# A quarter of the pair products laid with the batch on the partitions and summed by ScalarE and GpSimd

## The chip, the cores and the metric

The kernel runs on one core of a Trainium2 chip. The time is the device time of one execution in microseconds (us). The kernel before was timed at a median of 256.03 us over three runs (255.77 to 256.83). The profile is one more execution on the chip, with the instructions, DMA packets and semaphore events of that core.

## What is computed

It is a recommendation tower. For each of 512 samples, 32 table rows of 64 numbers are looked up. Each of the 496 pairs of fields has its own 64x64 matrix, and the pair gives one number per sample. These 496 numbers go through a linear layer, and then through a small network.

```python
e = jnp.stack([tbl_0[ids[:, 0]], ..., tbl_31[ids[:, 31]]], axis=1)      # 512 x 32 x 64
p = e[:, rows, :]; q = e[:, cols, :]                                    # rows, cols = triu_indices(32, k=1)
pij = jnp.einsum('bpe,dpe,bpd->bp', p, kernel, q)                       # kernel: 64 x 496 x 64, pij: 512 x 496
z = pij @ W.T + b                                                       # 256 wide
h = jnp.concatenate([z, dense_ctx], axis=1)                             # 272 wide
h = jnp.maximum(h @ W_top1 + b_top1, 0.0)                               # 512 wide
h = jnp.maximum(h @ W_top2 + b_top2, 0.0)                               # 256 wide
y = h @ W_top3
```

## The kernel before

**Layout.** The 32 fields are taken two at a time as 16 chunks. In `x_sb` a chunk is 128 partitions (two fields of 64 features) by 512 samples. Fields of chunks 0 to 3 come from small tables and are picked by one-hot matmuls (line 322), whose one-hots VectorE and ScalarE build (lines 543, 460, 463). The rows of chunks 4 to 15 are gathered by GpSimd with indirect DMAs into `gathered`, with 128 samples on the partitions: eight gathers for a chunk, 96 in all (line 280). After each of them GpSimd runs a memset of `rest_sb` (line 287), and it waits until the gather before the last has landed. TensorE then turns a chunk with four transposes (line 334, `turn`), and ScalarE copies it to `x_sb` and `own_sb` (lines 482, 486).

**The product groups.** The pairs are cut into tiles of two pairs and into 124 groups of two tiles. A group takes two matmuls (lines 351, 352), one on the upper and one on the lower half of the array rows, with the pair matrices in `k_sb` as the weights and 512 samples of `x_sb` as the moving operand. They fill one of three double banks of `t_ps`. VectorE multiplies the bank by `x_sb` of the other field into `prod` (line 556), a ring of six. Each such product still has to be summed over 64 features, which lie on the partitions. So after every four groups (`RUN`) TensorE runs two `reduce` calls of four matmuls (line 372) with a 0/1 selector; they accumulate in `sum_ps`. Every 16 such calls make a window, which ScalarE keeps in `pair_sums` (line 468). Four groups, those of fields inside a set of four chunks, have four smaller matmuls instead (lines 355 to 360).

**The order.** `plan()` writes out one order of steps, "fill c" (bring in chunk c) and "group g", and each engine walks it. TensorE works strictly in that order: a `turn` whose rows have not landed holds every group behind it, also those of earlier chunks. Chunk c is turned up to `LEAD` = 3 groups before its first group. The chunks' first groups are 7, 11, 16, 22, 30, 38, 47, 57, 69, 81, 94 and 108 for chunks 4 to 15. After the last group come the linear layer (line 379), the last two reduce calls, and the network (lines 405 to 431).

A product may start when VectorE has finished with the bank three products back (`prod_ready`), and the pieces of `k_sb` are loaded by SyncE, paced by the gathers.

Of the kernel before, what the change touches and what calls it, by code (L numbers as in the profile page):

```python
# [10 lines left out]
ALU = mybir.AluOpType  # L11
ACT = mybir.ActivationFunctionType

P = 128
# [31 lines left out]
GROUP = []  # L46
for c in range(CHUNKS):
    across = [(c, False, [[(i, 2 * c), (i, 2 * c + 1)] for i in (2 * a, 2 * a + 1)]) for a in range(c)]
    within = [(c, True, [[(2 * a + 1, 2 * a), (2 * a + 2, 2 * a + 3)] for a in (c - 3, c - 1)])] if c % SET == SET - 1 else []
    at = (1 - len(GROUP)) % RUN  # L50
    GROUP += across[:at] + within + across[at:]
GROUPS = len(GROUP)
NT = 2 * GROUPS
WITHIN = [g for g in range(GROUPS) if GROUP[g][1]]
FIRST_GROUP = [min(g for g in range(GROUPS) if GROUP[g][0] == c) if c else 0 for c in range(CHUNKS)]

BLOCK, BLOCK_OF = [], []
for g, (_, within, tiles) in enumerate(GROUP):  # L60
# [15 lines left out]
REDUCES = NT // COLS  # L76
# [4 lines left out]
G_RING = 8  # L81
LEAD = 3
# [19 lines left out]
def plan():  # L102

    steps, chunks = [], 0
    for g in range(GROUPS):
        while chunks < CHUNKS and (chunks < max(2, ONE_HOTS) or g >= FIRST_GROUP[chunks] - min(LEAD, (chunks - 1) // 2)):
            steps.append(("fill", chunks))
            chunks += 1
        steps.append(("group", g))
    return steps  # L110


def build(nc, ids, ids_t, iota, pick, tables, kern, w_pairs, b_int, ctx_rows, w_ctx_rows, w1, b1, w2, b2, w3, ident, selector, out):
    steps = plan()
    with ExitStack() as ctx:
# [18 lines left out]
        pair_sums = sb("pair_sums", [P, WINS, BATCH])  # L134

# [69 lines left out]
        window_kept = sem("window_kept")  # L205
        z_done = sem("z_done")
# [60 lines left out]
        def _(pool):  # L267
            pool.memset(w3_wide[:], 0.0).then_inc(w3_cleared, 1)
            pool.wait_ge(ids_in, 16)
            for n in range(CHUNKS - ONE_HOTS):  # L270
                if n >= G_RING:
                    pool.wait_ge(filled, n - G_RING + ONE_HOTS + 1)
                for f in range(2):
                    field = FIELD[2 * (n + ONE_HOTS) + f]
                    for t in range(BT):
                        k = (2 * n + f) * BT + t
                        landed = k - FLIGHT
                        if landed >= 0:
# [8 lines left out]
                        pool.memset(rest_sb[:], 0.0).then_inc(rested, 1)  # L287

        @block.tensor
        def _(pe):  # L290
# [35 lines left out]
            def turn(c):  # L326
# [6 lines left out]
                for t in range(BT):  # L333
                    mm = pe.transpose(tp_ps[:, t * P:(t + 1) * P], gathered[:, n % G_RING, t], ident_sb[:])  # L334
# [295 lines left out]
```

## Time and profile before

| | |
|---|---|
| Median of three runs | 256.03 us (255.77 to 256.83) |
| Profiled execution | 255.97 us |
| Its span, first to last instruction | 254.2 us |
| TensorE busy | 243.8 us, 96% |
| VectorE busy | 183.6 us, 72% |
| ScalarE busy | 50.5 us, 20% |
| GpSimd busy | 136.9 us, 54% |

The 1.77 us between the execution and its span lie around the first and the last instruction. The span has three parts: the picks with one-hots up to about 44 us, the product groups from there to 226.3 us, and the layers to the end. PE is TensorE, PEld its weight loads, DVE VectorE, ACT ScalarE and POOL GpSimd. The idle time of an engine counts only if another one, or the end, waits for it.

### The profile page before, as it was taken

To read this page: it belongs to the slowest core of one execution; us is meant where nothing else is said; L and a number is where in the kernel's file an instruction comes from. 1 tells how busy PE (TensorE), PEld (TensorE's weight loads), DVE (VectorE), ACT (ScalarE), POOL (GpSimd) and SP (SyncE) were. 2 spreads that over 40 slices of the span, in tenths; PEclk is the share of its full clock that TensorE was granted. 3 is DMA by queue.
4 is the path that set the end of the run, shared out by engine and by line. 5 is a ranking of instruction groups with operands and counts; after the bars stand their busy time and mean duration, and the time that the engine had idled before them with its cause. 6 is when DMAs were issued, how large, how long until landed. Compare 5 with 4: busy or idle time off the path is not lost.

```text
span 254.2 us, 3686 instructions
## 1 busy us (share of the span) xinstructions
PE 243.8 (96%) x1378; PEld 93.8 (37%) x1378; DVE 183.6 (72%) x205; ACT 50.5 (20%) x86; POOL 136.9 (54%) x197
## 2 busy tenths in 40 slices
PE   7778799999999999999999999999999999999996
PEld 3443454333332333333323333333333323333474
DVE  1999996867778687887768788788778768870130
ACT  3768677111110102010100200100100100001121
POOL 5766988888888888878888878700000000000000
PEclk9799999999999999999999999999999999999999
DMA  6294322333323333333333331182000000000000
GB/s 168 57 279 114 83 60 73 82 85 81 76 77 78 86 84 75 77 77 83 83 75 83 72 84 34 21 274 49 0 1 3 0 0 3 0 0 0 0 3 0
DMA packets 11028, 16.38 MB, mean 64 GB/s; under 512 B 5166, under 2 KB 5810, under 8 KB 11010
## 3 DMA queue, kind: packets, MB, share of 16 engines
q1 hardware_dynamic: 7768, 12.97, 18.0%
q0 software_dynamic: 3072, 3.15, 6.8%
q8 instruction: 11, 0.18, 0.3%
q10 hardware_dynamic: 170, 0.03, 0.1%
q14 instruction: 7, 0.06, 0.1%
HBM read 16.13 MB, written 0.00 MB: 63 GB/s over the span
## 4 chain that ended last, share of the span: by engine, by line
PE 91%; ACT 3%; issue 3%; DVE 2%; DVEq 0%
PE t_ps L351 43%; PE sum_ps L372 23%; PE sum_ps L322 5%; PE tp_ps L322 3%; PE t_ps L412 3%; PE tp_ps L334 3%; ACT distance L460 2%; PE t_ps L355 2%; PE t_ps L359 2%; PE tp_ps L379 2%; PE sum_ps L295 1%; PE t_ps L421 1%; PE t_ps L379 1%; PE t_ps L352 1%; ACT own_sb L486 1%
## 5 line engine op out<-in xcount | busy, mean ns | idle before, releaser
L556 DVE TENSOR_TENSOR prod<-t_ps,x_sb 128x1024 f32<-128x1024 f32 x120 | 139.3, 1218 | 33.4 <-PE t_ps L352 32.8
L351 PE MATMUL t_ps<-x_sb,k_sb 64*128 64x512 f32 x240 | 113.4, 606 | 0.4 <-ACT own_sb L486 0.4
L352 PE MATMUL t_ps<-x_sb,k_sb 64*128 64x512 f32 x240 | 113.5, 607 | 0.0
L280 POOL DMA_INDIRECT gathered<-in_tbl,ids_sb x96 | 94.7, 987 | 26.8 <-issue 13.0
L351 PEld LDWEIGHTS t_ps<-x_sb,k_sb 64*128 64x128 f32 x240 | 41.4, 186 | 63.1 <-issue 37.6
L372 PE MATMUL sum_ps<-prod,sel_sb 128*32 128x512 f32 x496 | 59.6, 598 | 0.0
L287 POOL MEMSET rest_sb<- 128x380 f32 x96 | 42.0, 438 | 0.1
L352 PEld LDWEIGHTS t_ps<-x_sb,k_sb 64*128 64x128 f32 x240 | 41.4, 186 | 0.0
L482 ACT COPY x_sb<-tp_ps 128x512 f32<-128x512 f32 x14 | 8.2, 586 | 107.1 <-PE tp_ps L334 104.2
L372 PEld LDWEIGHTS sum_ps<-prod,sel_sb 128*32 128x32 f32 x496 | 12.9, 109 | 42.3 <-issue 21.3
L543 DVE TENSOR_SCALAR pair_sums<-ids_bc,iota_sb 125x512 bf16<-125x512 f16 x57 | 24.3, 488 | 2.5 <-ACT ids_bc L444 2.1
L322 PE MATMUL tp_ps<-pair_sums,k_sb 125*64 125x512 bf16 x72 | 16.1, 411 | 4.3 <-DVE pair_sums L543 1.5
L322 PE MATMUL sum_ps<-pair_sums,k_sb 125*64 125x512 bf16 x76 | 14.6, 382 | 1.7 <-DVE pair_sums L543 1.0
L468 ACT COPY pair_sums<-sum_ps 128x512 f32<-128x512 f32 x4 | 2.3, 585 | 68.7 <-PE sum_ps L372 68.7
L460 ACT ACTIVATE distance<-ids_bc,iota_sb 125x512 f16<-125x512 f16 x17 | 12.1, 713 | 1.8 <-PE tp_ps L322 1.7
L463 ACT ACTIVATE pair_sums<-distance 125x512 bf16<-125x512 f16 x17 | 10.7, 630 | 0.5
L556 DVE TENSOR_TENSOR prod<-t_ps,own_sb 128x1024 f32<-128x1024 f32 x4 | 4.9, 1224 | 8.1 <-PE t_ps L360 8.1
L322 PEld LDWEIGHTS tp_ps<-pair_sums,k_sb 125*64 125x64 bf16 x72 | 6.7, 116 | 10.8 <-DVE pair_sums L543 3.4
L322 PE MATMUL tp_ps<-pair_sums,prod 125*64 125x512 bf16 x36 | 10.2, 411 | 0.0
L322 PE MATMUL sum_ps<-pair_sums,prod 125*64 125x512 bf16 x38 | 9.2, 379 | 0.0
L322 PEld LDWEIGHTS sum_ps<-pair_sums,k_sb 125*64 125x64 bf16 x76 | 5.8, 109 | 7.7 <-ACT pair_sums L463 2.2
L334 PEld LDWEIGHTS tp_ps<-ident_sb,gathered 128*128 128x128 f32 x48 | 5.0, 140 | 9.5 <-issue 9.5
(56 smaller groups left out, 117.5 us busy)
## 6 DMA issues: line engine op xcount, KB each, us to landing
k_sb<-in_kern SPq DMA_DIRECT2D x112, 64.0 KB, 2.1
gathered<-in_tbl,ids_sb POOLq DMA_INDIRECT x96, 2.6
k_sb<-in_tbl SPq DMA_DIRECT2D x5, 280.0 KB
k_sb<-in_kern SPq DMA_DIRECT2D x4, 256.0 KB, 4.0
w_sb<-in_w SPq DMA_DIRECT2D x2, 512.0 KB, 5.0
k_sb<-in_tbl SPq DMA_DIRECT2D x3, 224.0 KB
w_pairs_sb<-in_w_pairs SPq DMA_DIRECT2D x1, 512.0 KB, 3.4
ctx_sb<-in_ctx_rows SPq DMA_DIRECT2D x1, 192.0 KB, 5.5
```

The source lines that it names most:

```text
L280: pool.indirect_dma_start(gathered[:, n % G_RING, t, f * EMB:(f + 1) * EMB], None, tables[field], bass.IndirectOffsetOnAxis(ap=ids_sb[:, t ...
L287: pool.memset(rest_sb[:], 0.0).then_inc(rested, 1)
L322: mm = pe.matmul(bank[half:half + EMB, :], part[:, f, r, :], one_hot[:, n % OH_RING, :], start=(r == 0 and part is high_sb), stop=(r == PI ...
L334: mm = pe.transpose(tp_ps[:, t * P:(t + 1) * P], gathered[:, n % G_RING, t], ident_sb[:])
L351: pe.matmul(t[:, 0, :], k_sb[low, k, :], x_sb[low, a, :], start=True, stop=True)
L352: pe.matmul(t[:, 1, :], k_sb[high, k, :], x_sb[high, a, :], start=True, stop=True).then_inc(t_ready, 1)
L372: mm = pe.matmul(sum_ps[32 * j:32 * j + 32, :], sel_sb[:, 30 - 2 * k:62 - 2 * k], prod[:, (t // 2) % PROD_RING, t % 2, :], start=(k == 0), ...
L460: act.activation(distance[:, k % 2, :], ids_bc[:, f, :], ACT.Abs, scale=-1.0, bias=iota_sb[:, PICK[f][1] + r:PICK[f][1] + r + 1]).then_inc ...
L463: act.activation(one_hot[:, n % OH_RING, :], distance[:, k % 2, :], ACT.Relu, scale=-1.0, bias=1.0).then_inc(one_hot_ready_a, 1)
L482: act.copy(x_sb[:, n, :], from_ps[:]).then_inc(x_ready, 1)
L543: dve.tensor_scalar(one_hot[:, n % OH_RING, :], ids_bc[:, f, :], iota_sb[:, PICK[f][1] + r:PICK[f][1] + r + 1], None, ALU.is_equal).then_i ...
L556: dve.tensor_tensor(prod[:, g % PROD_RING], t_ps[:, g % T_RING], q, ALU.mult).then_inc(prod_ready, 1)
```

## The change

Chunks 4 to 7 are called near, chunks 0, 1 and 8 to 13 far. The pairs of a near with a far chunk, 32 of the 120 chunk pairs, leave the groups and become 32 side units: one for each far chunk and each quarter of the batch. In a side unit the operands of the matmuls change places. The weights are 128 samples of `x_sb`, and the moving operand is four blocks of `k_sb`, 512 columns. The result has the batch on the partitions. VectorE multiplies it by the near chunks' rows as gathered, which for that reason stay in four slots of `gathered` for good; the later chunks share the other four (`gathered_slot`), so a gather now waits for the turn of four chunks back. The features then lie along the free dimension, so no reduce matmul is needed. They are summed in `side_prod`, a ring of three: for 18 units by ScalarE with 16 ACTIVATEs that have an accumulator output (`sum_side`), for 14 of the last 20 by GpSimd with six halving additions, behind all its gathers. The sums of all units, 128 columns for each quarter, are turned once (`turn_side_sums`), just ahead of the last group, and kept in `pair_sums`.

So there are 92 groups and 32 side units, and 46 reduce calls where there were 62. The side units stand one behind every fourth group from group 15 on, and from group 62 on four among five groups. The first groups of chunks 4 to 15 are now 7, 9, 12, 16, 22, 26, 31, 37, 45, 53, 62 and 76, and `LEAD` is 5.

```diff
+NEAR = [4, 5, 6, 7]
+FAR = [0, 1, 8, 9, 10, 11, 12, 13]
...
+LEAD = 5
+SIDE_AT = [g for g in range(15, 63, RUN)] + [62 + 5 * k // 4 for k in range(SIDE_UNITS - 12)]
+SIDE = [(c, t) for c in FAR for t in range(BT)]
+BY_POOL = [m for m in range(12, SIDE_UNITS) if m % 3 != 2]
+BY_ACT_SUM = [m for m in range(SIDE_UNITS) if m not in BY_POOL]
+def plan():
+    steps, chunks, side = [], 0, 0
+    for g in range(GROUPS):
+        while chunks < CHUNKS and (chunks < max(2, ONE_HOTS) or g >= FIRST_GROUP[chunks] - min(LEAD, (chunks - 1) // 2)):
+            steps.append(("fill", chunks))
+            chunks += 1
+        steps.append(("group", g))
+        while side < SIDE_UNITS and SIDE_AT[side] <= g:
+            steps.append(("side", side))
+            side += 1
+        if g == GROUPS - 2:
+            steps.append(("side sums", 0))
+    return steps
...
-REDUCES = NT // COLS
+REDUCES = 2 * GROUPS // COLS
-G_RING = 8
-LEAD = 3
+G_RING = len(NEAR) + 4
+SIDE_RING = 3
+def gathered_slot(n):
+    return n if n < len(NEAR) else len(NEAR) + (n - len(NEAR)) % (G_RING - len(NEAR))
@@ gpsimd
-                    pool.wait_ge(filled, n - G_RING + ONE_HOTS + 1)
+                    pool.wait_ge(filled, n - (G_RING - len(NEAR)) + ONE_HOTS + 1)
+            halvings = 0
+            for m in BY_POOL:
+                c, t = SIDE[m]
+                k = FAR.index(c)
+                pool.wait_ge(prod_ready, UNITS.index(("side", m)) + 1)
+                part = side_prod[:, m % SIDE_RING].rearrange("p s (n e) -> p (s n) e", e=EMB)
+                for width in (32, 16, 8, 4, 2):
+                    if halvings:
+                        pool.wait_ge(halved, halvings)
+                    pool.tensor_tensor(part[:, :, 0:width], part[:, :, 0:width], part[:, :, width:2 * width],
+                                       ALU.add).then_inc(halved, 1)
+                    halvings += 1
+                pool.wait_ge(halved, halvings)
+                pool.tensor_tensor(side_sums[:, t, 16 * k:16 * k + 16], part[:, :, 0], part[:, :, 1],
+                                   ALU.add).then_inc(side_summed_p, 1)
@@ tensor
+            def side_products(m):
+                c, quarter = SIDE[m]
+                u = UNITS.index(("side", m))
+                k = SIDE_BLOCK_OF[c]
+                if quarter == 0:
+                    weights_in(k, len(NEAR))
+                    pe.wait_ge(x_ready, 2 * (c + 1))
+                pe.wait_ge(prod_ready, u - T_RING + 1)
+                t = t_ps[:, u % T_RING]
+                cols = slice(quarter * P, (quarter + 1) * P)
+                low, high = slice(0, EMB), slice(EMB, P)
+                pe.matmul(t[:, 0, :], x_sb[low, c, cols], k_sb[low, k:k + len(NEAR), :].rearrange("p g m -> p (g m)"),
+                          start=True, stop=True)
+                pe.matmul(t[:, 1, :], x_sb[high, c, cols], k_sb[high, k:k + len(NEAR), :].rearrange("p g m -> p (g m)"),
+                          start=True, stop=True).then_inc(t_ready, 1)
+            def turn_side_sums():
+                pe.wait_ge(side_summed_a, len(BY_ACT_SUM))
+                pe.wait_ge(side_summed_p, len(BY_POOL))
+                pe.wait_ge(x_ready, 2 * CHUNKS)
+                for t in range(BT):
+                    mm = pe.transpose(tp_ps[:, t * P:(t + 1) * P], side_sums[:, t, :], ident_sb[:])
+                mm.then_inc(side_turned, 1)
@@ scalar
+            def sum_side(m):
+                c, t = SIDE[m]
+                k = FAR.index(c)
+                act.wait_ge(prod_ready, UNITS.index(("side", m)) + 1)
+                for n in range(16):
+                    part = side_prod[:, m % SIDE_RING, n // 8, n % 8 * EMB:(n % 8 + 1) * EMB]
+                    one = act.activation(part, part, ACT.Copy, accum_out=side_sums[:, t, 16 * k + n:16 * k + n + 1])
+                one.then_inc(side_summed_a, 1)
@@ vector
+                if kind == "side":
+                    t = SIDE[g][1]
+                    if g >= SIDE_RING:
+                        user = g - SIDE_RING
+                        if user in BY_POOL:
+                            dve.wait_ge(side_summed_p, BY_POOL.index(user) + 1)
+                        else:
+                            dve.wait_ge(side_summed_a, BY_ACT_SUM.index(user) + 1)
+                    q = gathered[:, 0:len(NEAR), t, :].rearrange("p (o c) n -> p o c n", o=1)
+                    dve.tensor_tensor(side_prod[:, g % SIDE_RING].rearrange("p s (c n) -> p s c n", c=len(NEAR)),
+                                      t_ps[:, u % T_RING].rearrange("p s (c n) -> p s c n", c=len(NEAR)),
+                                      q.broadcast_to([P, 2, len(NEAR), P]), ALU.mult).then_inc(prod_ready, 1)
+                    continue
```

TensorE in the kernel before, the last stretch ahead of the turn of chunk 9 (the L334 row); L351 with L352 is one group, L372 x8 are two reduce calls:

```order
231 L351 MATMUL t_ps<-x_sb,k_sb 128x512
232 L352 MATMUL t_ps<-x_sb,k_sb 128x512
233 L351 MATMUL t_ps<-x_sb,k_sb 128x512
234 L352 MATMUL t_ps<-x_sb,k_sb 128x512
235 L351 MATMUL t_ps<-x_sb,k_sb 128x512
236 L352 MATMUL t_ps<-x_sb,k_sb 128x512
237 L351 MATMUL t_ps<-x_sb,k_sb 128x512
238 L352 MATMUL t_ps<-x_sb,k_sb 128x512
239 L372 MATMUL sum_ps<-prod,sel_sb 32x512 x8
240 L351 MATMUL t_ps<-x_sb,k_sb 128x512
241 L352 MATMUL t_ps<-x_sb,k_sb 128x512
242 L334 MATMUL tp_ps<-ident_sb,gathered 128x128 x4
```

There, 35 products stood ahead of this turn. TensorE in the changed kernel, from the turn of chunk 8 to that of chunk 9 (L413 is the turn, L460 and L461 a group, L434 and L436 a side unit, L481 the reduce calls):

```order
207 L413 MATMUL tp_ps<-ident_sb,gathered 128x128 x4
208 L460 MATMUL t_ps<-x_sb,k_sb 128x512
209 L461 MATMUL t_ps<-x_sb,k_sb 128x512
210 L434 MATMUL t_ps<-k_sb,x_sb 128x512
211 L436 MATMUL t_ps<-k_sb,x_sb 128x512
212 L460 MATMUL t_ps<-x_sb,k_sb 128x512
213 L461 MATMUL t_ps<-x_sb,k_sb 128x512
214 L460 MATMUL t_ps<-x_sb,k_sb 128x512
215 L461 MATMUL t_ps<-x_sb,k_sb 128x512
216 L481 MATMUL sum_ps<-prod,sel_sb 32x512 x8
217 L413 MATMUL tp_ps<-ident_sb,gathered 128x128 x4
```

Now four products, and no longer eight, lie between these two turns, and 24 stand ahead of the second. The turns of chunks 7, 8, 10, 11, 12, 13, 14 and 15 have 13, 20, 30, 37, 47, 57, 68 and 91 products ahead of them, where they had 19, 27, 44, 54, 66, 78, 91 and 105.

GpSimd's queue ended with a gather and a memset. In the changed kernel the halvings stand behind these; the first of them:

```order
197 L343 DMA gathered<-in_tbl,ids_sb 128x64
198 L350 MEMSET rest_sb 128x380
199 L361 ISA
200 L361 TENSOR_TENSOR side_prod<-side_prod 128x16x32
201 L361 TENSOR_TENSOR side_prod<-side_prod 128x16x16
202 L361 TENSOR_TENSOR side_prod<-side_prod 128x16x8
203 L361 TENSOR_TENSOR side_prod<-side_prod 128x16x4
204 L361 TENSOR_TENSOR side_prod<-side_prod 128x16x2
205 L365 TENSOR_TENSOR side_sums<-side_prod 128x16
```

Six additions are one side unit's sums, and 14 such sets stand there.

## Rows read from the trace of the kernel before

**Rows 1.** The page's first two parts: busy time, and 40 slices of the span.
```profile
PE 243.8 (96%) x1378; PEld 93.8 (37%) x1378; DVE 183.6 (72%) x205; ACT 50.5 (20%) x86; POOL 136.9 (54%) x197
...
PE   7778799999999999999999999999999999999996
...
PEclk9799999999999999999999999999999999999999
```

**Rows 2.** The chain that ended last, in order of time: start us, us, what.
```profile
106.30 1.85 PE sum_ps L372 x16
108.15 0.62 PE t_ps L351
108.78 0.42 PE t_ps L351
...
110.07 0.59 PE tp_ps L334 x4
...
112.57 1.85 PE sum_ps L372 x16
114.43 0.62 PE t_ps L351
...
118.06 1.85 PE sum_ps L372 x16
```

**Rows 3.** The same chain, turns of chunks 8, 9 and 11, a within group, and the last step.
```profile
80.76 0.57 PE t_ps L355
...
85.68 0.59 PE tp_ps L334 x4
...
97.45 0.59 PE tp_ps L334 x4
...
125.40 0.59 PE tp_ps L334 x4
...
226.31 2.77 PE tp_ps L379 x6
```

**Rows 4.** GpSimd's gathers (L280) alone, by stretches: us, POOL busy (gathers issued), PEclk, DMA.
```profile
0.00:61.50 61.50, 33.73 (x32) 0.97 0.42 109
0.00:86.90 86.90, 49.06 (x48) 0.98 0.39 100
0.00:99.30 99.30, 56.71 (x56) 0.98 0.39 98
0.00:112.90 112.90, 64.32 (x64) 0.98 0.38 96
0.00:125.40 125.40, 71.93 (x72) 0.99 0.37 94
```

**Rows 5.** GpSimd in order of time, and gathers from issue to landing (min, median, max).
```profile
84.26 0.95 POOL L280 DMA_INDIRECT gathered<-in_tbl,ids_sb  x1 [0.17 <-issue]
85.21 0.43 POOL L287 MEMSET rest_sb<- 128x380 f32 x1
86.01 0.95 POOL L280 DMA_INDIRECT gathered<-in_tbl,ids_sb  x1 [0.37 <-DMA gathered<-in_tbl,ids_sb]
...
111.90 0.95 POOL L280 DMA_INDIRECT gathered<-in_tbl,ids_sb  x1 [0.27 <-DMA gathered<-in_tbl,ids_sb]
...
DMA to landing us min/median/max: 2.4/2.6/6.1
```

**Rows 6.** VectorE in order of time: start us, us, what.
```profile
121.02 4.62 DVE L556 TENSOR_TENSOR prod<-t_ps,x_sb 128x1024 f32<-128x1024 f32 x4 [0.87 <-PE t_ps L352]
127.10 1.22 DVE L556 TENSOR_TENSOR prod<-t_ps,x_sb 128x1024 f32<-128x1024 f32 x1 [1.46 <-PE t_ps L352]
```

**Rows 7.** All engines by stretches: us, PE, PEld, DVE, ACT, POOL busy (instructions), PEclk.
```profile
8.00:9.00 1.00, 0.49 (x2) 0.32 (x3) 1.00 (x2) 1.00 (x4) 1.00 (x2) 0.83 0.00 0
9.00:12.00 3.00, 3.00 (x14) 1.62 (x13) 2.96 (x8) 2.02 (x4) 2.67 (x4) 0.50 0.14 22
12.00:15.00 3.00, 2.79 (x24) 1.77 (x21) 2.97 (x7) 2.49 (x4) 2.69 (x4) 0.99 0.83 246
251.00:254.20 3.20, 0.65 (x10) 0.39 (x8) 0.00 (x0) 0.27 (x1) 0.00 (x0) 1.00 0.00 1
```

**Rows 8.** Instructions by line and shape: count, busy us, mean ns of one, idle before.
```profile
L287 POOL MEMSET rest_sb<- 128x380 f32 x96 | 42.0, 438 | 0.1
L268 POOL MEMSET w_wide<- 128x64 f32 x1 | 0.2, 151 | 0.3 <-POOLq L622 0.3
L505 ACT COPY y_sb<-t_ps 128x128 f32<-128x128 f32 x1 | 0.3, 265 | 1.3 <-PE t_ps L431 1.3
L494 ACT COPY w_wide<-w_sb 128x2 f32<-128x2 f32 x1 | 0.2, 198 | 0.0
```

More of the change, by code:

```diff
@@ L41, with is_side, side_tile @@
 OH_RING = 8
-GROUP = []
+NEAR = [4, 5, 6, 7]
+FAR = [0, 1, 8, 9, 10, 11, 12, 13]
+SIDE_TILES = 8 * len(FAR)
+SIDE_GROUPS = SIDE_TILES // 2
+SIDE_UNITS = BT * len(FAR)
+def is_side(c, a):
+    return c in FAR and a in NEAR or c in NEAR and a in FAR
+def side_tile(k, s, n):
+    return 4 * (8 * (k % 2) + 4 * s + n) + k // 2
+side_tiles = {side_tile(k, s, n): [(2 * c + s, 2 * near), (2 * c + s, 2 * near + 1)]
+              for k, c in enumerate(FAR) for s in range(2) for n, near in enumerate(NEAR)}
@@ L51 @@
[L51 to L60, printed above, removed]
+    at = (1 - len(MAIN)) % RUN
+    MAIN += across[:at] + within + across[at:]
+GROUPS = len(MAIN)
+GROUP += MAIN
+NT = 2 * len(GROUP)
+WITHIN = [g for g in range(GROUPS) if MAIN[g][1]]
@@ new lines @@
+FIRST_GROUP = [min(g for g in range(GROUPS) if MAIN[g][0] == c) if c else 0 for c in range(CHUNKS)]
+LEAD = 5
[16 more added lines that the diff above has]
+    return steps
@@ new lines @@
+STEPS = plan()
+UNITS = [step for step in STEPS if step[0] in ("group", "side")]
+UNIT_OF_GROUP = [UNITS.index(("group", g)) for g in range(GROUPS)]
+BLOCK, BLOCK_OF, SIDE_BLOCK_OF = [], [], {}
+for kind, n in UNITS:
+    if kind == "side":
+        c, t = SIDE[n]
+        if t == 0:
+            SIDE_BLOCK_OF[c] = len(BLOCK)
+            BLOCK += [tuple((side_tile(FAR.index(c), s, k), (0, 1), 2 * c + s) for s in range(2)) for k in range(len(NEAR))]
+        continue
+    _, within, tiles = MAIN[n]
+    g = SIDE_GROUPS + n
@@ L99, in reduced_after @@
     return range(max(0, (g - RUN - 1) // 2), (g - 1) // 2) if g % RUN == 1 else range(0)
[L102 to L110, printed above, removed]
+def gathered_slot(n):
+    return n if n < len(NEAR) else len(NEAR) + (n - len(NEAR)) % (G_RING - len(NEAR))
 def build(nc, ids, ids_t, iota, pick, tables, kern, w_pairs, b_int, ctx_rows, w_ctx_rows, w1, b1, w2, b2, w3, ident, selector, out):
-    steps = plan()
+    steps = STEPS
     with ExitStack() as ctx:
@@ L333, in turn, with weights_in @@
                 for t in range(BT):
-                    mm = pe.transpose(tp_ps[:, t * P:(t + 1) * P], gathered[:, n % G_RING, t], ident_sb[:])
+                    mm = pe.transpose(tp_ps[:, t * P:(t + 1) * P], gathered[:, gathered_slot(n), t], ident_sb[:])
                 mm.then_inc(filled, 1)
+            def weights_in(k, blocks):
+                for s in range(SLICES):
+                    if k <= s * KS < k + blocks:
+                        pe.wait_ge(k_in[s], 16 * (2 if s < PIECES_FROM else PIECES))
@@ L339, in products @@
                 k = BLOCK_OF[g]
[L340 to L344 removed]
+                u = UNIT_OF_GROUP[g]
+                weights_in(k, 1 + within)
+                if u >= T_RING:
+                    pe.wait_ge(prod_ready, u - T_RING + 1)
                 if g == FIRST_GROUP[c]:
@@ L390, in _ @@
                         turn(n)
+                elif kind == "side":
+                    side_products(n)
+                elif kind == "side sums":
+                    turn_side_sums()
                 else:
```

61 lines of the change are left out of this document (37 added, 24 removed).

## The prediction

> **What bounds the kernel now.** I read the busy shares and slices first [rows 1]: TensorE is busy in every slice from the seventh to the last but one, at the full clock, so time is won only where TensorE loses work, and lost wherever it waits. Then the chain that ended last [rows 2]: TensorE alone, in a pattern. From one pair of reduce calls to the next without a turn it is 118.06 - 112.57 = 5.49 us, for four products. Inside, records follow at 0.43 us, two to a product, so a **product** is 0.857 us and four are 3.43. The **pair of reduce calls** is the rest, 2.06 us (1.85 of matmuls, and 0.20 by which the first record behind it, 0.62, is longer than the others' 0.42). With a turn the cycle is 112.57 - 106.30 = 6.27 us, so a **turn** is 0.78 us. VectorE needs 4.62 us for four multiplications in a row and 1.22 for one [rows 6], so they follow at 1.13 us. It fits four into 5.49 us and is not the bound. Last I read what feeds the turns, GpSimd's gathers [rows 4, 5]: they run from the start at a pace of their own, 0.95 us + 0.43 of memset + 0.17 and now and then a wait for a landing, some 13 us for a chunk's eight. At 86.9 us 48 are issued, which is chunks 4 to 9; the last of them went out at 86.01 and lands 2.6 us later, at about 88.7. TensorE turns chunk 9 at 97.45 [rows 3], 8.8 us later. So today the gathers are early, and that margin is not large.
>
> **What is saved.** Products: 32 groups go, 32 side units come, each again with two matmuls of 512 columns on half the rows, and I price one like a group, 0.857 us. Reduce calls: 62 become 46, eight pairs, 8 x 2.06 = 16.5 us off TensorE. The turn of the side sums adds 0.78. Taken alone, the span would be 254.2 - 16.5 + 0.8 = 238.5 us.
>
> **Where it goes: the turns come before their rows.** The order gives the products ahead of each turn. Chunk 9 has 24 ahead of it, where it had 35. In the kernel before, TensorE stood at product 24 shortly ahead of the within group at 80.8 us [rows 3]; now it has one turn more behind it at that point and short waits for the rows of chunks 7 and 8, so it arrives at about 82. The rows land at 88.7. Nothing in the change touches the pace of the gathers: the same 96, the same memsets, and the new wait for the turn of four chunks back is first met by chunk 12, for the turn of chunk 8, long past by then. **Chunk 9** holds TensorE 6.6 us, whatever happened before. From its turn (0.78, to 89.5) six products and one pair of reduce calls are 5.14 + 2.06, so TensorE stands at chunk 10 at 96.7; that chunk's last gather, the 56th, is issued by 99.3 [rows 4], about 98.5, and lands at 101.1: **4.4 us** of wait. To chunk 11 seven products and one pair, 0.78 + 6.00 + 2.06, so 109.9; its last gather went out at 111.90 and lands at 114.5: **4.6 us**. Chunk 12 comes ten products and two pairs later, a within group among them, at about 129.6, and its 72 gathers are all issued by 125.4 and landed by about 127; from there the rows are in time.
> So the turn of chunk 11 stands at 114.6 us. Before it was at 125.40, and 226.31 - 125.40 = 100.9 us later the groups were done [rows 3]; in these were 70 products, 17 pairs of reduce calls, five turns and two within groups. Now 87 products, 15 pairs, the same turns and within groups, and the turn of the side sums are left: 100.9 + 17 x 0.857 - 2 x 2.06 + 0.78 = 112.2 us. The groups end at 226.8 us: **0.5 us later than before**. The whole 16.5 us are spent in waits for rows.
>
> **The dense stretch.** From group 62 on, four side units stand among five groups, so seven products (once eight) lie between reduce pairs where there were four. TensorE makes one in 0.857, VectorE takes one in 1.13, and there are three banks. A pair of reduce calls lets VectorE catch up. Counted from its end, VectorE is done with the first product at 1.06 (0.857 and the longer start) + 0.1 + 1.22 = 2.4 us, and then every 1.13. TensorE needs a bank for its sixth product at 4.49 and gets it at 4.66, a wait of 0.17; the seventh and the eighth wait 0.27 each. Five stretches of 0.44 and one of 0.71 make 2.9 us, less where a turn lies between: **2.7 us**. Bounds: 0, if the three banks smooth it, and 5, if a multiplication by `gathered` with its broadcast takes 0.1 us more, which no row shows.
>
> **The clock.** The granted clock fell to its lower level (1.2 of 2.4 GHz) once in the kernel before, from about 8.7 to 12.1 us, behind a pause of 1.3 us and light work, and 9 to 12 us reads 0.50 [rows 7]. After the last matmul it stays at 1.00 to the end of the span. Pauses of 6.6, 4.4 and 4.6 us are none that a row shows, and I expect it to fall in the first and in the third. What is lost behind the first is taken back from the wait at chunk 10, but behind chunk 11 nothing absorbs it: 3.4 us at half rate cost **1.7 us**. Bounds 0 and 3.4 (twice the stretch). The Trainium skill, TensorE: Matmul & The Clock Gate, Part 1, says that the throttled state is the default and activity releases it; by this the fall is certain in the long pause, and the sum would stay as it is.
>
> **The sums.** No row shows an addition of GpSimd or an accumulating ACTIVATE. *GpSimd*: memsets of 380 and 64 elements take 438 and 151 ns [rows 8], so 0.91 ns an element and 93 ns fixed. Six additions write 512 + 256 + 128 + 64 + 32 + 16 = 1008 elements: 0.9 us, and six times 93 ns and a 0.17 us gap [rows 5], 1.6 us, make 2.5 us as the low end; with two reads and a write in turn, three times the element time, 4.3. I take 3.9, nearer the end that moves two operands. Three side units come with 6.75 products and 0.94 pairs of reduce calls, 8.0 us with small waits, and GpSimd has two of the three, so it keeps up to **4.0 us** a unit, and 3.9 is just covered by the products. The last two side units both belong to it; six products' time behind them is not quite enough for both: **0.6 us** at the turn of the side sums. Of GpSimd, the Trainium skill, GPSIMD Engine Reference, 3.1 and 4.1, says that a two-input elementwise operation is about twice as slow as on VectorE, and that one belongs there: 4.5 us for 2048 elements. By that figure a unit would be an estimated 3.8 us, the sum would be about the same, and the margin to 4.0 is that thin.
> *ScalarE*: copies of 128 and 2 columns take 265 and 198 ns [rows 8], so 64 columns about 232 ns. Sixteen are 3.7 us, and with a second instruction of 198 ns to bring out each accumulator 6.9. It gets one side unit in 6.35 us up to group 59, beside two copies of some 1.2 us for each chunk, so up to about 5.8 it costs nothing. I take 4.5, and nothing. At 6.9 it would cost 4 us.
>
> **The sum.** 254.2 + 0.5 + 2.7 + 1.7 + 0.6 = 259.7 us of span, and with the 1.77 around it **261.5 us**. The profiled execution (255.97) is as good as the median (256.03), so it stands as it is: +2.1%.
>
> **The rivals.**
> *The sums bind.* If a GpSimd unit takes 5 us, 14 of them are 70 us. The first starts when side unit 12 is multiplied, at about 169 us, so the last is done at 239; with the turn of the side sums and the last group the groups end at 241, where the forecast has 231.8: 9 us more, 271 us. It decides from 4.0 us a unit up; my price lies at 3.9, and the ring of three hands the delay to VectorE and then to TensorE. ScalarE at 7 us is the smaller form, 265. For it speaks how narrow both margins are, against it that the low ends lie well under them. Chance 0.22.
> *The waits for rows and little else.* VectorE's and the clock's terms vanish: 254.2 + 0.5, with 1.77 around it 256.5 us, no change that a measurement of this kernel can tell (about 0.5%). Chance 0.15.
> *The rows are in time*, and it is faster: the eight pairs are saved, the dense stretch costs its 2.7, so 238.5 + 2.7 + 1.8 = 243.0 us. The place is the turns of chunks 9 to 11, and it decides where GpSimd issues a chunk's gathers in under 8.5 us and not in 13. The pace of 1.55 us a gather does not depend on TensorE, so a gain of this size is hardly to be had; a pace a little quicker, less disturbed by landings (0.37 where a row shows it), would give 2 or 3 us. Chance 0.07 for all that ends under 254.7.
> The forecast, from 257.3 to 266, has the rest, 0.56.
>
> **How the numbers follow.** Likeliest is 261.5 us. The low end of the range, 256.0, takes in the case with the waits alone; the high end, 272, the known bounds together (5 for VectorE, 3.4 for the clock, 4 for ScalarE, some 3 for GpSimd at 4.3: 254.2 + 0.5 + 15.4 + 1.8 = 271.9) and part of the case in which the sums bind. Faster by over 0.5%: 0.07; within 0.5%: 0.14; slower: 0.79.
>
> **What the profile after would show.** Right: TensorE idle ahead of the turns of chunks 9, 10 and 11 by about 6.6, 4.4 and 4.6 us, released by gathers; the turn of chunk 11 at 114.6; an unchanged pace of gathers; 46 reduce calls; short waits for VectorE behind 165 us, and VectorE near 98% there; a lower clock around 89 or 115 us; the layers starting near 232. Wrong: turns of chunks 9 to 11 without idle time; a TensorE wait of many us at the side sums, or VectorE waiting for GpSimd, would mean that the sums bind; side units longer than 0.857 us would be a cost that I have put at nothing.

## The result, and the profile after

The changed kernel takes 263.2 us (median of four runs, 261.15 to 263.57) against 255.9 us (255.14 to 256.83): a ratio of 1.028, with a 95% interval of 1.024 to 1.032. It is slower. The profiled execution has a span of 261.4 us, 7.2 more than before.

The page's first two parts, as in [rows 1]:

```profile
PE 236.9 (91%) x1254; PEld 92.1 (35%) x1254; DVE 182.7 (70%) x205; ACT 120.8 (46%) x662; POOL 182.5 (70%) x281
...
PE   7788799998986395949999999999999999999996
...
PEclk9799999999999779979999999999999999999999
```

TensorE has 124 matmul records fewer and is busy 6.9 us less, but three notches stand in its row, between the 13th and the 18th slice (78 to 118 us), where the kernel before had none. The clock's row has notches behind the first and the last. TensorE in order of time around the turn of chunk 9 (start us, us, what, and in brackets the idle time and who ended it), and the part of all idle time ahead of the turns between 81 and 116 us:

```profile
81.02 1.92 PE L481 MATMUL sum_ps<-prod,sel_sb 128*32 128x512 f32 x16
89.00 1.08 PE L413 MATMUL tp_ps<-ident_sb,gathered 128*128 128x128 f32 x4 [6.05 <-DMA gathered<-in_tbl,ids_sb]
...
  DMA gathered<-in_tbl,ids_sb: 12.5, 3
```

These are the three waits at the turns of chunks 9 to 11, and they end with a gather's landing. Two short ones, of 1.0 and 0.7 us, stand at chunks 7 and 8. Answering to [rows 4], the gathers alone by stretches:

```profile
0.00:61.50 61.50, 33.15 (x31) 0.97 0.41 108
0.00:86.90 86.90, 48.83 (x48) 0.98 0.39 100
0.00:112.90 112.90, 64.14 (x64) 0.95 0.37 95
0.00:125.40 125.40, 71.31 (x72) 0.95 0.36 93
```

They are where they were, to one gather, so the rows arrive when they did before, and TensorE comes for them earlier. The chain that ended last says the same. Before, it was 91% TensorE; now it is this:

```profile
PE 55%; DMA 21%; POOL 19%; issue 4%; ACT 0%
PE t_ps L460 21%; DMA gathered<-in_tbl,ids_sb 20%; POOL gathered L343 13%; PE sum_ps L481 11%; PE t_ps L434 10%; POOL rest_sb L350 6%; PE t_ps L526 3%; PE tp_ps L488 1%; PE t_ps L535 1%; PE tp_ps L413 1%; PE t_ps L488 1%; PE t_ps L464 1%; PE t_ps L468 1%; DMA ids_sb<-in_ids 1%; PE tp_ps L535 1%
```

Up to the turn of chunk 11 the chain runs through GpSimd and its gathers, behind it through TensorE alone. It passes that turn at 114.99 us, and the layers start at 233.56 (226.31 before):

```profile
114.99 1.09 PE tp_ps L413 x4
...
161.09 1.85 PE sum_ps L481 x16
167.59 1.85 PE sum_ps L481 x16
176.35 1.85 PE sum_ps L481 x16
185.12 1.85 PE sum_ps L481 x16
...
229.00 1.85 PE sum_ps L481 x16
231.91 0.59 PE tp_ps L444 x4
233.56 2.77 PE tp_ps L488 x6
```

The clock, answering to [rows 7], by stretches (us, then PE, PEld, DVE, ACT, POOL busy, and PEclk):

```profile
84.00:88.00 4.00, 0.00 (x0) 0.00 (x0) 0.00 (x0) 0.88 (x8) 3.51 (x6) 0.96 0.35 88
88.00:94.00 6.00, 5.00 (x14) 2.58 (x16) 1.38 (x2) 1.17 (x2) 5.49 (x8) 0.50 0.32 77
...
115.00:118.00 3.00, 3.00 (x10) 1.64 (x12) 0.00 (x0) 2.98 (x21) 2.67 (x5) 0.50 0.28 68
118.00:120.00 2.00, 2.00 (x18) 0.54 (x18) 1.87 (x2) 0.24 (x1) 1.83 (x3) 0.91 0.42 105
```

And the new operations, by line and shape (mean ns of one behind the busy us):

```profile
L591 ACT ACTIVATE side_prod<-side_prod 128x64 f32<-128x64 f32 x288 | 69.1, 241 | 66.4 <-DVE side_prod L686 58.5
L591 ACT ACTIVATION_READ_ACCUMULATOR side_prod<-side_prod 128x1 f32 x288 | 53.9, 187 | 0.0
L686 DVE TENSOR_TENSOR side_prod<-t_ps,gathered 128x1024 f32<-128x1024 f32 x32 | 38.9, 1216 | 3.1 <-PE t_ps L436 3.1
L361 POOL TENSOR_TENSOR side_prod<-side_prod 128x512 f32<-128x512 f32 x14 | 17.8, 1272 | 15.0 <-DVE side_prod L686 15.0
L361 POOL TENSOR_TENSOR side_prod<-side_prod 128x256 f32<-128x256 f32 x14 | 10.3, 735 | 1.1
L365 POOL TENSOR_TENSOR side_sums<-side_prod 128x16 f32<-128x16 f32 x14 | 3.0, 217 | 1.1
```

The multiplication by `gathered` takes 1216 ns, as that by `x_sb` does. ScalarE and GpSimd sat waiting for VectorE for 58.5 and 15.0 us, and nobody is shown waiting for them.

### The profile page after: what moved, and what is told of

The parts are those of the page before. It is cut to its first block, busy times and chain, and to the rows that moved or that the text cites. A ratio compares the mean times of both kernels' runs of the same rounds, so it can differ in the third digit from the quotient of the medians.

```text
span 261.4 us, 4114 instructions
## 1 busy us (share of the span) xinstructions
PE 236.9 (91%) x1254; PEld 92.1 (35%) x1254; DVE 182.7 (70%) x205; ACT 120.8 (46%) x662; POOL 182.5 (70%) x281
## 4 chain that ended last, share of the span: by engine, by line
PE 55%; DMA 21%; POOL 19%; issue 4%; ACT 0%
PE t_ps L460 21%; DMA gathered<-in_tbl,ids_sb 20%; POOL gathered L343 13%; PE sum_ps L481 11%; PE t_ps L434 10%; POOL rest_sb L350 6%; PE t_ps L526 3%; PE tp_ps L488 1%; PE t_ps L535 1%; PE tp_ps L413 1%; PE t_ps L488 1%; PE t_ps L464 1%; PE t_ps L468 1%; DMA ids_sb<-in_ids 1%; PE tp_ps L535 1%
## 5 line engine op out<-in xcount | busy, mean ns | idle before, releaser
L699 DVE TENSOR_TENSOR prod<-t_ps,x_sb 128x1024 f32<-128x1024 f32 x88 | 104.4, 1217 | 39.0 <-PE t_ps L461 31.3
L591 ACT ACTIVATE side_prod<-side_prod 128x64 f32<-128x64 f32 x288 | 69.1, 241 | 66.4 <-DVE side_prod L686 58.5
L460 PE MATMUL t_ps<-x_sb,k_sb 64*128 64x512 f32 x176 | 92.0, 631 | 0.1
L461 PE MATMUL t_ps<-x_sb,k_sb 64*128 64x512 f32 x176 | 92.1, 632 | 0.0
L361 POOL TENSOR_TENSOR side_prod<-side_prod 128x512 f32<-128x512 f32 (+4 forms) x70 | 42.5, 607 | 19.4 <-DVE side_prod L686 15.0
L591 ACT ACTIVATION_READ_ACCUMULATOR side_prod<-side_prod 128x1 f32 x288 | 53.9, 187 | 0.0
L460 PEld LDWEIGHTS t_ps<-x_sb,k_sb 64*128 64x128 f32 x176 | 30.5, 192 | 48.5 <-issue 26.1
L481 PE MATMUL sum_ps<-prod,sel_sb 128*32 128x512 f32 x368 | 44.3, 598 | 0.0
L686 DVE TENSOR_TENSOR side_prod<-t_ps,gathered 128x1024 f32<-128x1024 f32 x32 | 38.9, 1216 | 3.1 <-PE t_ps L436 3.1
L434 PE MATMUL t_ps<-k_sb,x_sb 64*128 64x512 f32 x64 | 34.2, 614 | 0.0
L436 PE MATMUL t_ps<-k_sb,x_sb 64*128 64x512 f32 x64 | 34.2, 614 | 0.0
L461 PEld LDWEIGHTS t_ps<-x_sb,k_sb 64*128 64x128 f32 x176 | 30.5, 192 | 0.0
L413 PE MATMUL tp_ps<-ident_sb,gathered 128*128 128x128 f32 x48 | 8.7, 308 | 14.5 <-DMA gathered<-in_tbl,ids_sb 14.2
L481 PEld LDWEIGHTS sum_ps<-prod,sel_sb 128*32 128x32 f32 x368 | 9.6, 109 | 31.5 <-issue 24.3
L401 PE MATMUL tp_ps<-pair_sums,k_sb 125*64 125x512 bf16 x72 | 15.6, 410 | 3.9 <-DVE k_sb L652 1.5
L434 PEld LDWEIGHTS t_ps<-k_sb,x_sb 64*128 64x128 f32 x64 | 11.3, 190 | 19.3 <-issue 10.1
L413 PEld LDWEIGHTS tp_ps<-ident_sb,gathered 128*128 128x128 f32 x48 | 5.6, 153 | 24.1 <-issue 22.9
```

Source lines behind the costliest of these rows:

```text
L361: pool.tensor_tensor(part[:, :, 0:width], part[:, :, 0:width], part[:, :, width:2 * width], ALU.add).then_inc(halved, 1)
L401: mm = pe.matmul(bank[half:half + EMB, :], part[:, f, r, :], one_hot[:, n % OH_RING, :], start=(r == 0 and part is high_sb), stop=(r == PI ...
L434: pe.matmul(t[:, 0, :], x_sb[low, c, cols], k_sb[low, k:k + len(NEAR), :].rearrange("p g m -> p (g m)"), start=True, stop=True)
L436: pe.matmul(t[:, 1, :], x_sb[high, c, cols], k_sb[high, k:k + len(NEAR), :].rearrange("p g m -> p (g m)"), start=True, stop=True).then_inc ...
L460: pe.matmul(t[:, 0, :], k_sb[low, k, :], x_sb[low, a, :], start=True, stop=True)
L461: pe.matmul(t[:, 1, :], k_sb[high, k, :], x_sb[high, a, :], start=True, stop=True).then_inc(t_ready, 1)
```

## The experiments

The theory was that the changed kernel loses at the places where TensorE comes to a turn before the rows, with small parts for the dense stretch and the clock. The main rival was that the sums on ScalarE and GpSimd bind through the ring of three.

### Do the sums bind?

The first run leaves out nearly all of the sums, and with them the sum over the 64 features:

```diff
-                for n in range(16):
-                    part = side_prod[:, m % SIDE_RING, n // 8, n % 8 * EMB:(n % 8 + 1) * EMB]
-                    one = act.activation(part, part, ACT.Copy, accum_out=side_sums[:, t, 16 * k + n:16 * k + n + 1])
+                part = side_prod[:, m % SIDE_RING].rearrange("p s (n e) -> p (s n) e", e=EMB)
+                one = act.copy(side_sums[:, t, 16 * k:16 * k + 16], part[:, :, 0])
...
-                for width in (32, 16, 8, 4, 2):
...
```

> The features of the side units are not summed: ScalarE copies one column of 64 (one instruction for a unit and not 32), GpSimd adds two columns (one addition and not six). So it leaves out nearly all of the sums' work. If the sums are hidden, the time is that of the changed kernel to 0.5 us, 262.5 to 263.5. If they bind, it falls by several us, towards 255.

Measured: 262.55 us (262.24 to 264.49), where the changed kernel has 263.2. ScalarE's share is now 18 copies of 219 ns and GpSimd's 14 additions of 214 ns, and the time is the same within the spread of the runs. So the sums are hidden. The opposite, all of the last 20 units on GpSimd:

```diff
-BY_POOL = [m for m in range(12, SIDE_UNITS) if m % 3 != 2]
+BY_POOL = [m for m in range(12, SIDE_UNITS) ]
```

> The changed kernel with all of the last 20 side units summed by GpSimd, where ScalarE had six of them. One unit takes GpSimd 3.64 us, and in the dense stretch a side unit comes every 2.66 us. If the ring of three hands that on, the last sums are ready 20 x 3.64 = 73 us after 173, at 246, and the groups end 13 to 14 us later than in the changed kernel: 275 to 278 us. This is the rival in which the sums bind, made to happen. If TensorE hides it, the time stays at 263.

Measured: 277.59 us (275.99 to 279.16), ratio 1.088. TensorE and GpSimd near the end, in order of time:

```profile
233.58 0.69 PE L460 MATMUL t_ps<-x_sb,k_sb 64*128 64x512 f32 x1 [1.33 <-DVE side_prod L686]
243.04 1.05 PE L444 MATMUL tp_ps<-ident_sb,side_sums 128*128 128x128 f32 x4 [4.29 <-issue]
...
239.34 3.30 POOL L361 TENSOR_TENSOR side_prod<-side_prod 128x512 f32<-128x512 f32 x5
242.72 0.21 POOL L365 TENSOR_TENSOR side_sums<-side_prod 128x16 f32<-128x16 f32 x1
```

GpSimd works without a pause at one unit in 3.6 us, VectorE waits for a slot of the ring, TensorE for VectorE, and the side sums are turned when the last addition is done. This is what the rival looks like. Some 1.5 us of the loss, by an estimate, is a fall of the clock behind the wait of 4.29 us (granted 0.51 from 243 to 246 us). In the changed kernel GpSimd had two units of three, 7.2 us of work in about 8.8 (the 8.76 us from 167.59 to 176.35 hold three side units), and the rival did not occur.

### Are the waits for rows the loss?

The turns back to where they were relative to their groups:

```diff
-LEAD = 5
+LEAD = 3
```

> The changed kernel with LEAD = 3 as before and not 5: the turns of chunks 9, 10 and 11 stand one, one and two groups later, the last with a pair of reduce calls between. The gathers are as they were. If the place of the turns against the rows is what costs, the work that then stands ahead of the turn of chunk 11 is 3.8 us more and the time 259.5 to 261 us. If the waits don't matter, it stays at 263, and if ScalarE's copies come too late with less lead, it is slower.

Measured: 258.54 us (257.20 to 259.83), ratio 1.012: 4.7 us less by this alone, a little more than expected. The turns of chunks 9 and 10 still wait, 5.5 and 2.3 us, and those of chunks 7 and 8 wait 2.1 and 1.2; that of chunk 11 no longer does. It starts at 115.6 us, 0.6 later than before this edit, but with two more products and a pair of reduce calls (3.8 us) done. The clock does not fall behind it either, which the expectation had left out and which is worth some 1.6 us (see below).

The side units spread evenly:

```diff
-SIDE_AT = [g for g in range(15, 63, RUN)] + [62 + 5 * k // 4 for k in range(SIDE_UNITS - 12)]
+SIDE_AT = [15 + 9 * k // 4 for k in range(SIDE_UNITS)]
-BY_POOL = [m for m in range(12, SIDE_UNITS) if m % 3 != 2]
+BY_POOL = [m for m in range(18, SIDE_UNITS) if m % 3 != 2]
```

> The changed kernel with its side units spread evenly, one behind every 2.25 groups from group 15 to 84, and GpSimd's share starting at unit 18. Gathers and memsets are as they were. Three more products stand ahead of the turn of chunk 11, in time that TensorE waited anyway (2.6 us less to do later), and there is no stretch in which more than six products stand between two pairs of reduce calls (2 to 3 us less). If these two places are where the time lies, it is 257 to 259.5 us, still slower than before since the waits stay. If ScalarE, which now gets a unit every 4 us and needs 3.9, binds instead, it is 262 or more.

Measured: 257.22 us (255.27 to 261.67 over ten runs), ratio 1.004 (1.000 to 1.008). The waits at the turns of chunks 9 to 11 fell from 12.5 to 8.5 us. The turn of chunk 11 starts at 113.2 us with three more products done. From there to the layers it is 113.4 us and not 118.6: 2.6 us for the three products, 1.7 for a clock that did not fall behind this turn (the wait was 1.4 us), and only 0.9 for the dense stretch. Of the 2 to 3 us expected from the latter less than half came, because stretches of six products lose too. The pairs of reduce calls of this kernel start at:

```profile
162.66 1.85 PE sum_ps L481 x16
170.38 1.85 PE sum_ps L481 x16
178.02 1.85 PE sum_ps L481 x16
184.61 1.85 PE sum_ps L481 x16
```

Six products and one pair, 7.20 us by their prices, take 7.72 and 7.64, and five (6.35) take 6.59.

### What does the clock cost?

Matmuls of zeros fill the waits:

```diff
                pe.wait_ge(x_ready, 2 * c)
+                for _ in range({9: 6, 10: 2, 11: 3}.get(c, 0)):
+                    pe.matmul(tp_ps[:], zeros[:, 0:P], zeros[:], start=True, stop=True)
```

> The changed kernel with idle matmuls of zeros in the waits: six, two and three of 0.86 us ahead of the waits for the rows of chunks 9, 10 and 11, each into the bank that the turn then writes. The rows come no earlier. If the lower clock behind the pauses costs its share, the clock stays at 1.00 and the time falls by 1.5 to 2 us, to 261 to 261.7. If the clock costs nothing, or if the matmuls delay the turns, it is 263 or more.

Measured: 261.4 us (259.95 to 262.61), ratio 1.023, 1.8 less than the changed kernel; the intervals of the two overlap, so the trace has to bear it out. By stretches:

```profile
84.00:88.00 4.00, 3.74 (x9) 1.33 (x7) 0.00 (x0) 0.33 (x3) 3.54 (x5) 1.00 0.39 92
88.00:94.00 6.00, 5.76 (x32) 2.44 (x36) 4.03 (x4) 1.67 (x7) 5.34 (x9) 1.00 0.34 76
...
100.00:106.00 6.00, 5.22 (x18) 2.48 (x20) 2.52 (x3) 1.15 (x3) 5.34 (x9) 0.72 0.31 75
...
115.00:120.00 5.00, 5.00 (x32) 1.69 (x30) 2.90 (x3) 3.79 (x22) 4.50 (x7) 1.00 0.33 79
```

The clock is up behind the turns of chunks 9 and 11. It fell once around chunk 10, where a pause of 2.4 us was left, and what that cost only shortened the slack ahead of chunk 11. From the turn of chunk 11 to the layers it is 116.9 us and not 118.6. That is the price of the fall behind chunk 11, 1.6 to 1.7 us.

### What sets the pace of the rows?

The memset between two gathers cut short, in both kernels:

```diff
-REST = 380
+REST = 4
```

> The memset between two gathers is 4 and no longer 380 elements wide, so a gather takes about 1.3 us of GpSimd and not 1.6; nothing else changes. If the turns of chunks 9 to 11 wait for rows whose pace GpSimd alone sets, the rows of chunk 9 are there by about 76 us, the three waits (6.0, 2.8, 3.6 us) and the fall of the clock behind them go, and the time is 244 to 247 us (the eight pairs of reduce calls saved, the dense stretch still costing 3 to 4 us). If the sums on ScalarE and GpSimd bind, the time stays at 261 to 263 us, with a long wait at the side sums.

> The control: the kernel before with the same short memset. There TensorE never waits for rows, so early rows are worth nothing: 255 to 257 us. If short memsets help or harm by themselves (contention of the gathers with other transfers or with VectorE), it shows here, as a difference of 1 us or more.

Measured: 259.71 us (258.44 to 260.29) for the changed kernel, and 252.29 us (252.15 to 252.44) for the one before, ratios 1.015 and 0.987. Here I was wrong. Both kernels gained some 3.5 us, because the picks run quicker and the groups start that much earlier (the turn of chunk 4 at 49.0 us and not 52.6 in the kernel before). The quicker part is VectorE's: its 57 one-hots in bf16 take 371 ns each beside the short memsets and 488 ns beside the long ones. The distance between the kernels stayed, 7.4 us, and so did the waits for rows (6.2, 2.2 and 3.8 us). The gathers and memsets of the kernel before with the short memset, by line:

```profile
L280 POOL DMA_INDIRECT gathered<-in_tbl,ids_sb x96 | 94.0, 979 | 52.3 <-DMA gathered<-in_tbl,ids_sb 42.5 <-issue 7.0 <-DMA ids_sb<-in_ids 2.2
L287 POOL MEMSET rest_sb<- 128x4 f32 x96 | 11.7, 122 | 0.1
```

The 30 us that the memsets gave up went into waits for landings, 42.5 us where there were 11.2. A gather lands 2.7 us after its issue (median), and with two allowed in flight the landings set the pace; the memset only hid it. So next four in flight, with the short memset:

```diff
-REST = 380
+REST = 4
-FLIGHT = 2
+FLIGHT = 4
```

> The changed kernel with the short memset (4 elements) and four gathers in flight where there were two (FLIGHT = 4). With the short memset alone GpSimd waited 43 us for landings, and the rows came no faster. If two in flight set the pace, it is now 0.95 + 0.12 + 0.19, some 1.3 us a gather; the rows of chunk 9 are there by about 70 us, the waits at the turns of chunks 9 to 11 go, and the clock stays up. Then the time is 240 to 245 us (238.5 of span for the saved reduce calls, 3 to 4 for the dense stretch, 1.8 around it, and 3 less because of the earlier start that the short memset gives both kernels). If the gathers' pace is set by the transfers themselves, each lands later and the time stays at 257 to 260 us.

> The control: the kernel before with the same two edits. With the short memset alone it took 252.3 us; its turns never wait for rows, so more gathers in flight change nothing: 251.5 to 253 us. If gathers in flight delay other transfers at the start, it is slower.

Measured: 334.58 us (333.61 to 338.95) and 348.81 us (348.54 to 352.16), ratios 1.31 and 1.37. Both expectations were wrong by far. The page of the kernel before with these two edits, and all its engines by stretches:

```profile
PE   8843312243488994088899999999999999999997
...
PEclk9965555555589998569899999999999999999999
DMA  5631110174320254303134000000000000000000
...
20.00:50.00 30.00, 10.12 (x21) 2.50 (x21) 3.91 (x7) 2.70 (x4) 25.60 (x48) 0.51 0.11 26
50.00:60.00 10.00, 1.97 (x5) 0.54 (x5) 0.73 (x2) 0.00 (x0) 5.94 (x11) 0.50 0.09 20
```

GpSimd issues at its 1.25 us, but while it does, from 20 to 50 us, the DMA engines are 11% busy and move 26 GB/s. Single picks of TensorE wait up to 7 us, at half clock. The turn of chunk 4, at 52.6 us in the kernel before, comes at 123.7. Is it the quicker issue or the allowance of four? The changed kernel with four allowed in flight and the long memset:

```diff
-FLIGHT = 2
+FLIGHT = 4
```

> Tells apart what made the two kernels with four gathers in flight and a short memset take 335 and 349 us: the changed kernel with four in flight, but the memset of 380 elements, so that a gather goes out every 1.55 us at most. If the depth of four is what harms, it is over 300 us as well. If the pace of 1.25 us was what harmed, it stays near 262 us, and a little under if the 12 us in which GpSimd waited for landings go.

Measured: 254.38 us (253.40 to 256.42 over ten runs), ratio 0.998 (0.994 to 1.002). The allowance alone does no harm, and the short memset alone does none; together they do. Which of pace and depth it is stays open: a gather every 1.55 us that lands 2.6 us after its issue rarely has more than one other beside it, so four at once were hardly reached here. How the other transfers are brought to a stand was not settled either. And the rows come earlier:

```profile
L343 POOL DMA_INDIRECT gathered<-in_tbl,ids_sb x96 | 95.2, 992 | 17.9 <-issue 15.6 <-DMA ids_sb<-in_ids 2.3
```

GpSimd no longer waits for landings (12.3 us in the changed kernel). The last gather of chunk 9 is issued at 80.4 us and not 86.5, the waits at the turns of chunks 9 to 11 are 0.8, 3.9 and 1.7 us, and the groups end 8.9 us earlier: 7.3 by which the turn of chunk 11 comes earlier (107.7 us), and 1.6 for the clock, which stays up behind it. One number, which touches no matmul and no sum, gives back all that the change had lost. This is the strongest evidence for the theory. The kernel before was not run with it; its turns never wait for rows, and the groups of the changed kernel started no earlier with it (turn of chunk 4 at 53.8 us, where it was 52.3), so there was nothing to be expected, but that is not shown.

### Versions that beat both

Here the side units are moved into the waits, with gathers and memset as they were. ScalarE is not quick enough for so many so early (3.9 us each), so VectorE takes four:

```diff
+SIDE_AT = [15, 17, 19, 20, 21, 21, 22, 24, 25, 26, 27, 28, 29, 30] + [33 + 3 * j for j in range(18)]
+BY_DVE = [3, 5, 8, 11]
+BY_POOL = [m for m in range(23, SIDE_UNITS) if m % 3 != 2]
...
+                    if g in BY_DVE:
+                        k = 16 * FAR.index(SIDE[g][0])
+                        dve.wait_ge(prod_ready, u + 1)
+                        dve.tensor_reduce(side_sums[:, t, k:k + 16], side_prod[:, g % SIDE_RING].rearrange("p s (n e) -> p (s n) e", e=EMB),
+                                          mybir.AxisListType.X, ALU.add).then_inc(side_summed_v, 1)
```

> The changed kernel with 14 side units (five before) ahead of the turn of chunk 11, and the other 18 one behind every third group. ScalarE alone could not sum the early ones, at 3.9 us each, so VectorE sums four of them with a tensor_reduce. Gathers and memsets are as they were. Six more products are made before the turn of chunk 9 can start and nine more before that of chunk 11, in time in which TensorE waited (12.4 us), and never more than seven products stand between two pairs of reduce calls, mostly five or six. If the loss lies in the waits for rows and in the dense stretch, it is 249 to 253 us, faster than the kernel before. If VectorE or ScalarE binds in the early stretch, it is 255 or more.

Measured: 251.09 us (250.25 to 252.63), ratio 0.983 (0.978 to 0.987). Of the waits one of 3.9 us at chunk 9 and one of 1.2 us at chunk 7 are left. A `tensor_reduce` of 128x1024 takes 1220 ns. Then earlier still, with seven sums on VectorE, `LEAD` = 3 and the short memset:

```diff
+SIDE_AT = [15, 15, 15, 20, 20, 21, 21, 22, 24, 25, 27, 28, 28, 32, 34, 38, 40, 43, 46, 52, 53, 55, 57, 57, 60, 61, 69, 70, 73, 78, 81, 85]
+BY_DVE = [1, 2, 3, 6, 8, 13, 16]
+BY_POOL = [23, 24, 26, 28, 29, 31]
-LEAD = 5
+LEAD = 3
-REST = 380
+REST = 4
```

> The same idea with the side units placed earlier still, seven sums on VectorE, LEAD = 3 (each turn from chunk 9 on one or two groups later) and the short memset, which started the groups of both kernels 3.5 us earlier. Taken together it should leave next to nothing of the waits: 243 to 248 us. Against the kernel before with the short memset (252.3) that would be the gain of the saved reduce calls, less what VectorE costs.

Measured: 247.56 us (median of four runs, 247.90, 247.73, 247.40 and 243.88), the fastest of all. By the medians the ratio is 0.970; 0.963 (0.953 to 0.972) comes from the two quickest runs alone. The page of it:

```profile
PE 231.8 (94%) x1254; PEld 90.8 (37%) x1254; DVE 184.4 (75%) x212; ACT 123.9 (50%) x694; POOL 126.0 (51%) x233
...
PE   7999789997799978699999999999999999999995
...
PEclk9999999999999999999999999999999999999999
```

The layers start at 218.2 us. The clock stays up. Against the kernel before with the short memset (252.3) the idea of the change is worth about 5 us by the medians, and not the 16.5 of the saved reduce calls: 6.5 us of waits for rows are left, and what VectorE costs. Four gathers in flight with the long memset and this placing together were not tried.

## Why the prediction was right

The forecast was 261.5 us in a range of 256 to 272; measured are 263.2. The mechanism is the one forecast. That the number is this near is in part luck: the turn of chunk 11 came 0.4 us later than forecast and the dense stretch cost 2.0 more, while the 0.6 at the side sums fell away. Term by term:

- **What bounds, and the prices.** Product 0.857, pair of reduce calls 2.06, turn 0.78: they hold. Side units run like groups, and the eight pairs are gone (368 reduce records for 496).
- **The waits for rows.** Forecast 6.6, 4.4 and 4.6 us at chunks 9, 10 and 11, 15.6 in all, and the turn of chunk 11 at 114.6. Measured 6.05, 2.81 and 3.60, 12.5 in all, and 114.99. The single waits are shorter: TensorE came to chunk 9 a little later than forecast, behind waits of 1.0 and 0.7 us at chunks 7 and 8, and later still to chunk 10 (99.7 us and not 96.7), mostly because of the clock's fall. The anchor, the landing of chunk 11's rows, was right to 0.4 us, and it alone counts. That the waits are the loss was only argued in the prediction. LEAD = 3, the even placing and above all four gathers in flight show it.
- **The clock.** Forecast: falls at the first and third wait, for 3.4 us each, 1.7 us lost behind the third. It fell at these two (0.50 from 88 to 94 and from 115 to 118), and the filled waits give 1.6 to 1.7 back. Behind the first it stayed down until about 94.5, over 5 us and not 3.4, which cost nothing, since the wait at chunk 10 took it up. Of the rule in the Trainium skill, TensorE: Matmul & The Clock Gate, Part 1, that activity releases the throttled state, the trace agrees: the clock was down behind the pauses of 6.0 and 3.6 us and not where matmuls of zeros filled them; behind the pause of 2.8 us between them it stayed up.
- **The dense stretch.** This term was mis-sized: 2.7 us, and about 4.7 measured (118.6 from the turn of chunk 11 to the layers, less 112.2 and 1.7 for the clock; the side sums waited for nothing). The chain shows seven products and a pair in 176.35 - 167.59 = 8.76 us, and 185.12 - 176.35 = 8.77, where the prices say 8.06: 0.70 a stretch, and I had 0.44. Five products lose 0.15 (167.59 - 161.09 = 6.50 against 6.35), where I had nothing. The mechanism is right, VectorE holding TensorE through three banks, but TensorE has to wait earlier than the count of banks says. VectorE, and TensorE's weight loads for the fifth, sixth and seventh product of that stretch:

```profile
171.70 1.22 DVE L686 TENSOR_TENSOR side_prod<-t_ps,gathered 128x1024 f32<-128x1024 f32 x1
172.96 0.18 PEld L460 LDWEIGHTS t_ps<-x_sb,k_sb 64*128 64x128 f32 x1 [0.71 <-DVE side_prod L686]
174.09 0.18 PEld L434 LDWEIGHTS t_ps<-k_sb,x_sb 64*128 64x128 f32 x1 [0.83 <-DVE prod L699]
175.22 0.18 PEld L460 LDWEIGHTS t_ps<-x_sb,k_sb 64*128 64x128 f32 x1 [0.83 <-DVE side_prod L686]
```

VectorE leaves the second product's bank at 172.92, and the load for the fifth starts 0.04 us later and takes 0.18. The wait for a bank stands ahead of the weight load and not only ahead of the matmul, so a bank has to be free some 0.22 us before its product is due. I had counted the bank as free to use at VectorE's end: by that the fifth product waits for nothing and the sixth 0.17, and measured are 0.15 and 0.27. This is read from the times of the trace; no run tried it. VectorE was not near 98% busy there, which I had named as a sign, but at 86 to 90% (13.5, 13.0 and 13.6 us in the stretches of 15 us from 175 to 220): behind each pair it waits 0.75 us for the next product.
- **The sums.** Forecast 3.9 us a GpSimd unit, measured 3.6 (173.00 to 176.58); forecast 4.5 on ScalarE, measured 3.9 (16 times 0.24, the accumulator's read of 187 ns overlapping the ACTIVATE). Both under the points from which they bind, 4.0 and 5.8. The 0.6 us at the side sums did not occur: the last addition ended at 230.9, the turn came at 231.9. The rival, at 5 us a unit, was forecast to cost 9; made to happen at a similar load, it cost 14.
- By the figure of the Trainium skill, GPSIMD Engine Reference, 3.1 (4497 ns for an addition of 2048 elements, 2.2 ns an element), a unit was an estimated 3.8 us. The trace agrees with this slope: from 256 to 512 elements it is 1272 - 735 = 537 ns, 2.1 ns an element.
- **The rival in which the rows come in time** I put at a gain of "2 or 3 us" for a pace less disturbed by landings. That was too low: without its waits for landings GpSimd brings chunk 9 6 us earlier, which is worth 8.8 us of time. I had read the waits of [rows 5] as single disturbances and not added them up: 11.2 us over the 96 gathers.

## What to carry to other kernels

Before taking work off an engine that is always busy, add up when each input it will ask for arrives: here 16.5 us of saved matmuls turned into 12.5 us of waits for rows that came exactly when they came before. If an engine works in a fixed order, work that needs nothing new must be placed ahead of the wait, where it is free; the same 32 side units in other places were worth 12 us (263.2 against 251.1). And a producer's pace has to be read with all that limits it: taking away one limit (the memset) uncovered the next (two in flight), and taking away both cost 71 us in the changed kernel and 93 in the one before.

## What the runs showed of the hardware

- With indirect gathers of 128 rows of 64 floats issued every 1.25 us and four allowed in flight, the other transfers came nearly to a stand: 26 GB/s and 11% DMA busy between 20 and 50 us, and 93 us more for the whole kernel before (348.8 against 255.9). Four allowed at one issue in 1.55 us (254.4, changed kernel, against 263.2) and the same short memset with two allowed (252.3, kernel before) are both faster than what they came from.
- An accumulating ACTIVATE is two instructions, 241 and 187 ns for 64 columns, but a pair follows the last after 0.24 us.
- VectorE's TENSOR_SCALAR of 125x512 to bf16 took 488 ns on average while GpSimd ran memsets of 380 elements between its gathers, and 371 ns with memsets of 4 (both in the kernel before).
- In these runs the length of a pause of TensorE did not settle by itself whether the granted clock fell behind it. It read 0.50 behind pauses of 2.4 us (even placing, 102 to 104 us) and 2.3 us (`LEAD` = 3, 105 to 107), and stayed at 1.00 behind one of 2.8 us in the changed kernel (102 to 107) and one of 2.2 us in the changed kernel with the short memset (100 to 104). Behind the waits for rows of 3.6 us and more it fell each time.
